# The attention output tile and the raw key buffer move in SBUF: same instructions, other addresses

## The reference, cut to what matters

```python
x = x + _L0_attn_ref(_layernorm(x), Wq, bq, ..., Wo, M, z)      # retrieval from a memory M, 8 heads of 128
x = x + _L0_xattn_ref(_layernorm(x), ctx, Wq, Wk, Wv, Wo)       # 32 query heads, 4 key/value heads
x = x + _L0_ffn_ref(_layernorm(x), router_w, router_b, expert_b) # softmax, top 8 of 64, mix of expert biases

# the part that the change touches, in _L0_xattn_ref:
out = jnp.einsum('bhgqk,bkhd->bqhgd', attn, v)
out = out.reshape(b, q_len, N_HEADS * HEAD_DIM)
return out @ Wo
```

## Time and profile before

| | us |
|---|---|
| three runs | 751.18, 752.24, 749.66; median 751.18 |
| span of the profiled execution, first to last instruction | 746.1 |
| TensorE matmul busy | 723.4 (97%) |
| VectorE busy | 417.2 (56%) |
| ScalarE busy | 352.9 (47%) |

### The profile page before, as it was taken

One profiled execution on the slowest core, in us unless ns is written; L12 is line 12 of the kernel. 1 busy time (PEld: TensorE's weight loads), 2 busy tenths in 40 slices (PEclk: granted clock), 3 DMA queues, 4 the chain that ended last, 5 costly groups with the idle time before them and its releaser, 6 DMA issues.

```text
span 746.1 us, 10784 instructions
## 1 busy us (share of the span) xinstructions
PE 723.4 (97%) x3644; PEld 596.5 (80%) x3644; DVE 417.2 (56%) x914; ACT 352.9 (47%) x1033; POOL 44.5 (6%) x47
## 2 busy tenths in 40 slices
PE   7998799999999999999999999999999999999996
PEld 5886678888888788888888888888888888888873
DVE  2575997676202445444565554464544446567885
ACT  3443685443324545444554454464544455444541
POOL 0026620000000000000000000000000000000000
PEclk9999999999999999999999999999999999999997
DMA  9847530012342231200041110023120001001001
GB/s 329 302 146 252 184 114 1 0 61 82 129 149 77 54 123 43 78 22 20 17 163 42 42 49 21 14 59 110 42 72 26 16 19 37 15 1 50 15 29 43
DMA packets 48546, 56.85 MB, mean 76 GB/s; under 512 B 3200, under 2 KB 29824, under 8 KB 48512
## 3 DMA queue, kind: packets, MB, share of 16 engines
q1 hardware_dynamic: 43904, 48.02, 20.4%
q10 hardware_dynamic: 4608, 8.39, 3.0%
HBM read 45.91 MB, written 10.49 MB: 76 GB/s over the span
## 4 chain that ended last, share of the span: by engine, by line
PE 90%; DVE 6%; ACT 1%; DMA 1%; issue 1%; SPq 0%; POOL 0%; ACTq 0%; DVEq 0%
PE bank L678 24%; PE bank L657 23%; PE bank L492 13%; PE bank L755 7%; PE bank L625 6%; PE bank L813 6%; PE bank L791 4%; PE bank L483 2%; PE bank L520 1%; DVE sig L1197 1%; PE bank L736 1%; DMA keys_dram<-kvout 1%; PE bank L717 1%; PE bank L566 1%; DVE kvout L1181 1%
## 5 line engine op out<-in xcount | busy, mean ns | idle before, releaser
L657 PE MATMUL bank<-xnT,regA 128*128 128x512 f32 x768 | 190.7, 398 | 0.0
L678 PE MATMUL bank<-regC,oT 128*128 128x512 f32 x768 | 184.7, 396 | 1.4 <-DVE oT L1101 1.4
L678 PEld LDWEIGHTS bank<-regC,oT 128*128 128x128 f32 x768 | 143.9, 188 | 36.0 <-DVE oT L1101 1.8
L657 PEld LDWEIGHTS bank<-xnT,regA 128*128 128x128 f32 x768 | 140.1, 188 | 28.6 <-issue 0.8
L1028 ACT ACTIVATE probs<-bank,negmax 128x128 f32<-128x128 f32 x256 | 89.8, 377 | 50.1 <-DVE negmax L1316 50.1
L1101 DVE TENSOR_TENSOR oT<-bank,oT 128x512 fp32r<-128x512 f32 x64 | 44.1, 691 | 71.1 <-ACT oT L840 71.0
L840 ACT CAST pT<-bank 128x512 fp32r<-128x512 f32 x64 | 34.5, 589 | 96.7 <-PE bank L791 96.7
L858 ACT ACTIVATE qT<-bank 128x512 f32<-128x512 f32 x64 | 39.3, 614 | 74.3 <-PE bank L657 74.3
L492 PE MATMUL bank<-regC,xnT 128*128 128x512 f32 x288 | 70.5, 396 | 0.0
L755 PEld LDWEIGHTS bank<-k_ring,qT 128*128 128x128 f32 x512 | 62.0, 191 | 3.8 <-ACT qT L858 1.1
L755 PE MATMUL bank<-k_ring,qT 128*128 128x128 f32 x512 | 62.4, 275 | 0.7 <-ACT qT L858 0.7
(11 more groups left out here) (110 smaller groups left out, 799.8 us busy)
## 6 DMA issues: line engine op xcount, KB each, us to landing
raw<-in_L_attn_Wo SPq DMA_DIRECT2D x8, 1024.0 KB, 5.6
raw<-in_L_xattn_Wo SPq DMA_DIRECT2D x4, 2048.0 KB, 9.3
wq_raw<-in_L_xattn_Wq SPq DMA_DIRECT2D x16, 512.0 KB, 4.3
k_ring<-keys_dram SPq DMA_DIRECT2D x32, 128.0 KB, 2.3
v_raw<-vals_dram SPq DMA_DIRECT2D x64, 64.0 KB, 2.3
rawk<-in_L_xattn_Wv SPq DMA_DIRECT2D x4, 512.0 KB, 4.0
rawk<-in_L_xattn_Wk SPq DMA_DIRECT2D x4, 512.0 KB, 8.3
resid<-in_x SPq DMA_DIRECT2D x4, 512.0 KB, 11.1
```

What stands on the lines that cost most here:

```text
L657: last = nc.tensor.matmul(k_bank[:, :], wq[:, a, head, c, :], xnT[:, b, c, half * HALF:(half + 1) * HALF], start=i == 0, stop=i == 3 * KC - 1)
L678: last = nc.tensor.matmul(bank[7][:, :], oT[:, parity, a, h, :], wo[:, b, h, :], start=h == 0 and i == 0, stop=h == GH - 1 and i == 2)
```

## The change

The declarations are reordered. `xnT` and `regA` come first; then `rawk` is declared in a stack that is closed at once, and `oT` takes its place; `regC` follows; `resid` and `raw16` come after `regC`. No instruction, semaphore or shape is touched.

```diff
-        resid = sb("resid", [P, NT, D])
         xnT = sb("xnT", [P, 2, KC, NTOK], R)
         regA = sb("regA", [P, 2, 4096], R)
+
+        lower = ExitStack()
+        rawk = sb("rawk", [P, 4096], F, lower)
+        lower.close()
+        oT = sb("oT", [P, 2, 2, GH, P], R)
         regC = sb("regC", [P, 2, 4096], R)
+
+
+        resid = sb("resid", [P, NT, D])
         raw16 = sb("raw16", [P, 4096])
...
         first = ExitStack()
         regB = sb("regB", [P, 2, 4096], R, first)
-        rawk = sb("rawk", [P, 4096], F, first)
...
         second = ExitStack()
         qT = sb("qT", [P, 2, 8, GH, S], F, second)
-        oT = sb("oT", [P, 2, 2, GH, P], R, second)
```

## The result

The changed kernel takes 743.99 us, the median of six runs (742.86 to 745.13), the kernel before 750.2 us over its six (747.98 to 752.24). The ratio is 0.9923, 95% interval 0.9899 to 0.9947: 5.8 us less, with 4.0 to 7.6 as the interval. Timed a second time (run g2) it was 0.9927 (0.9900 to 0.9953). The forecast was 746.1 us and 5.1 us less.

A forecast was written before the change was run, and what follows sets the result against it. TensorE's matmul pace was taken to bound the kernel. The projection's 5.3 us less 0.2 for starts, all other parts 0, gave a 741.0 us span, plus 5.1 to the median: 746.1 us, range 744.4 to 749.5.

The forecast's parts named there:

- TensorE alone bounds the attention stage: From 249 to 630 us TensorE is busy for 380.15 of 381.00 us, so only the matmuls' pace counts there.
- two paces at the same shape: 128x512 matmuls: quick 0.2266 us on pairs of xnT, regA, regC; slow 0.2335 us with regB or oT in the pair.
- both readings: Tiles are quick at multiples of 128 bytes, or below 131200; by either, oT's move makes the projection quick.
- 768 x 0.0069 = 5.3, less 0.2 for starts: 768 projection matmuls go from 0.2335 to 0.2266 us; five last-group cases lose 0.2 to starts, leaving 5.1 us.
- the start (0.5): Five last-group projections that follow the scores or a wait lose between nothing and 5 x 0.11 = 0.5 us.
- the last steps (0.7): In the last group, the projection gain of a few steps may be lost, 5 x 0.15 = 0.7 us at most.
- The second rival: Quick only where bases are a multiple of 32 KiB apart: projection stays slow, L492 loses 2.6 us, 753.8 us; chance 0.04.
- The first rival: A tile's place has no effect, the slow pace belongs to something else: nothing changes, 751.2 us; chance 0.10.
- The level: The median lies 5.1 us above the span, so a span of 741.0 us becomes a time of 746.1 us.

The follow-up runs named there:

- e1: Kernel before with 96 bytes of padding in front of oT and 32 behind, so oT stays high at a multiple of 128; 1.0016 of the kernel before.
- e2: Changed kernel with 32 bytes of padding in front of oT and 96 behind, so oT is low and not aligned; 1.0034 of the kernel before.
- f1: Kernel before with 224 bytes in front of oT and 288 behind: oT stays high, its distance to regC a multiple of 512; ratio 0.9947.
- g1: Changed kernel with 32 bytes of padding between xnT and regA, changing only the distances to xnT; ratio 0.9984.
- h1: The kernel before, unedited, profiled again; the end is at 746.5 us.
- e4: Changed kernel with 64 bytes of padding in front of oT and 64 behind; ratio 0.9988.
- f3: Changed kernel with 256 bytes of padding in front of oT and 256 behind; ratio 0.9955.
- f4: Changed kernel with 32 bytes of padding ahead of xnT, moving all tiles from xnT on together; ratio 0.9932.
- g3: Changed kernel with 224 bytes of padding ahead of both stage stacks, giving all operand tiles the same remainder; ratio 0.9911, median 743.18 us.
- e3: Changed kernel with 96 bytes of padding ahead of both stage stacks, so regB and regA are at multiples of 128; ratio 0.9935.

## Why the prediction was right, and where it wasn't

- *TensorE alone bounds the attention stage, so the pace of the matmuls reaches the end.* Right: 4.7 us less busy in L683, 4.9 us less from the first scores to the end, no new wait.
- *There are two paces at the same shape, and the pair of tiles decides.* Right, and it was legible before the change, from one function whose calls differ only in their tiles. Three kernels with oT at other places (e1, e2, f1) show it from both sides.
- *Which property of the pair.* Wrong in both readings, alignment of the tile and half of SBUF, and here the forecast was lucky. Both readings agreed with the change only because it happened to turn a distance of -82720 into one of 16384, a multiple of 256. Neither would have said where else to put the tile: e1 and e2 each followed one of them and gained nothing.
- *768 x 0.0069 = 5.3, less 0.2 for starts.* The rows give 24 x 32 at 0.2270 us instead of 0.2335: 5.0 us, within the reading of the rows. A slip in the bounds changed nothing: with the start (0.5) and the last steps (0.7) taken from 5.3 the lower end is 4.1, not 3.9 us.
- *The second rival*, that the distance counts, had the right quantity and the wrong period: 32 KiB instead of 256 bytes. xnT and regC went from 65536 to 81920 apart and kept their 21.92 us.
- *The first rival*, no effect of the place, is refuted by f1 and g1. The Trainium skill's rule that was weighed for it (SBUF — State Buffer, "Who interferes with whom": TensorE never waits on anyone) isn't tested between engines by any run here; between TensorE's own two operands the runs differ by 3% of a matmul's pace, and the measurement decides.
- *The level.* The forecast took the 5.1 us between span and median of before for what lies around an execution. h1 has 748.45 us with a span of 746.5, the changed kernel 745.13 with 743.0: about 2 us lie around it. The first profile of before was of an execution quicker than the median, and the median came down to 750.2 with more runs. The 2.1 us between forecast and result are these: 1.0 the base, 1.1 the larger measured gain, 6.2 us by the medians, which the interval of the ratio doesn't tell from 5.1.

What stays open: no run says why the period is 256 bytes. In every group here the weights being loaded and the rows in motion come from the same two tiles, so the runs don't say whether a matmul is held up by its own weights' place or by the next one's. A remainder of 192 wasn't tried, and only the 128x512 shape of `float32r` was followed.

## What to carry to other kernels

Where TensorE is the bound, read the pace of each 128x512 group from merged rows of the timeline and compare groups of one shape that follow matmuls of that shape; where they differ, work out the distance of their two tiles and pad it to a multiple of 256 bytes. Small tiles ahead of large ones (here 800 bytes of constants, 32 more than a multiple of 256) put every pair across them out of step, and padding put in for one pair moves all others, as e2 and e4 did. A placement that happens to work is not yet a rule: cross its properties one by one before giving it a reason.

## What the runs showed of the hardware that was not expected

The pace of back-to-back weight load and matmul of 128x512, by (length - 0.39) / (n - 1), against the remainder by 256 of the distance, moving less stationary:

| remainder | rows | us a matmul |
|---|---|---|
| 0 | projection after, f1, f3, f4, g1, g3; x96 before and after | 0.2270 (x24), 0.2266 (x96) |
| 32 | L625 before | 0.2335 |
| 64 | projection in e4 | 0.2291 |
| 96 | projection in e2 | 0.2339 |
| 128 | projection in e1, L631 in e3; x96 of L499 in e2, e4 | 0.2330, 0.2334 |
| 160 | L632 in e2 | 0.2343 |
| 224 | projection before; x96 in g1 | 0.2335, 0.2334 |

The last but one is from e2's own row:

```profile
129.23 5.78 PE L632 MATMUL bank<-regB,regA 128*128 128x512 f32 x24
```

A row is read to 0.01 us, which is 0.0004 us a matmul for 24: between 0.2330 and 0.2343 that is hardly a difference, while 0 and 64 stand clear of the rest. The same remainder gave the same pace on different tiles, lines and halves of SBUF.

The 12 queries of a step, even at remainder 0, take 3.00 to 3.02 us. The price is that of following shorter matmuls, and not of a new pair: in g2, the changed kernel, 12 matmuls that follow another pair of the same shape take 2.89 us, and 12 of the same pair behind transposes 3.01:

```profile
61.95 3.05 PE L497 MATMUL bank<-regA,regB 128*128 128x512 f32 x12
64.84 2.89 PE L497 MATMUL bank<-regC,xnT 128*128 128x512 f32 x12
...
67.67 0.60 PE L588 MATMUL bank<-ident,wofold 128*128 128x128 f32 x4
68.03 3.01 PE L497 MATMUL bank<-regC,xnT 128*128 128x512 f32 x12
```

When the groups around them are in step too, the queries behind the scores take 2.98 us instead of 3.02 (g3): a small part of the price goes with the distances.
